# Attention and ternary feed-forward block on one core: x's first load in quarters, q rotated on VectorE alone, and the places of values steps, ring slots and inverse transfers

## What is computed

```python
q, k, v = n(x) @ Wq, n(x) @ Wk, n(x) @ Wv          # n: layer norm; 256, 64 and 64 columns
q = rope(q, ang); k = rope(k, ang[:, :8])          # q over its 256 columns, k within each head
p = softmax(einsum('bhqd,bhkd->bhqk', q, k) / 16)
x = x + n(einsum('bhqk,bhkd->bhqd', p, v) @ Wo)
w = where(W > d, 1, where(W < -d, -1, 0)) * alpha  # d = 0.7 * mean(abs(W))
x = x + n(n(x) @ w.T + bias)
```

## Time and profile before

| | |
|---|---|
| median of three runs | 1492.5 us (1488.67 to 1494.1) |
| profiled execution, its own time | 1492.92 us |
| its span, first to last instruction | 1491.1 us |
| TensorE matmul busy | 1431.0 us (96%) |
| VectorE busy | 1337.7 us (90%) |
| ScalarE busy | 1240.0 us (83%) |
| GpSimd busy | 754.6 us (51%) |
| first product of maxima begins | 49.28 us |

### The profile page before, as it was taken

The page is one execution under the profiler, slowest core; times in us unless marked ns, Lnnn a source line. Parts: engine busy times, 40 slices in busy tenths (PEclk is TensorE's granted clock), DMA queues, the critical chain, the costliest instruction groups (busy, mean ns, idle before and its releaser), DMA issues.

```text
span 1491.1 us, 32225 instructions
## 1 busy us (share of the span) xinstructions
PE 1431.0 (96%) x12350; PEld 460.7 (31%) x12350; DVE 1337.7 (90%) x1471; ACT 1240.0 (83%) x2483; POOL 754.6 (51%) x1205
## 2 busy tenths in 40 slices
PE   6699999999999999999999999999999999999996
PEld 5122322223232332323222233323322232222236
DVE  5798999999999999999999999999999989999814
ACT  2079889898988989898898989898898989899881
POOL 4322275645665466745656555745656455363340
PEclk9589999999999999999999999999999999999999
DMA  3311121311212130221313122221311112121001
GB/s 106 102 48 48 33 71 41 98 34 50 70 60 66 51 80 23 87 53 46 79 36 94 31 72 48 78 63 41 76 41 55 39 60 66 36 66 31 30 23 44
DMA packets 72921, 84.92 MB, mean 57 GB/s; under 512 B 17632, under 2 KB 58464, under 8 KB 71328
## 3 DMA queue, kind: packets, MB, share of 16 engines
q1 hardware_dynamic: 71952, 82.08, 19.7%
q10 hardware_dynamic: 816, 0.79, 0.2%
HBM read 46.66 MB, written 24.64 MB: 48 GB/s over the span
## 4 chain that ended last, share of the span: by engine, by line
PE 73%; ACT 12%; DVE 7%; issue 4%; POOL 2%; DMA 1%; SPq 0%; POOLq 0%; ACTq 0%; DVEq 0%
PE pv L1017 28%; PE smax L995 27%; ACT probs L887 10%; DVE row_max L1267 5%; PE ring L1130 5%; PE ring L1041 3%; PE ring L1104 3%; PE ring L1118 2%; PE ring L1138 2%; ACT heads L951 1%; PE ring L1124 1%; PE ring L1065 1%; PE ring L1088 1%; ACT act L940 1%; PE smax L961 0%
## 5 line engine op out<-in xcount | busy, mean ns | idle before, releaser
L1267 DVE TENSOR_REDUCE row_max<-smax 128x1 f32<-128x1024 f32 x1024 | 1202.0, 1216 | 82.6 <-PE smax L995 73.1
L887 ACT ACTIVATE probs<-ring 128x512 f32<-128x512 f32 x2048 | 1103.9, 598 | 114.2 <-PE ring L1041 91.7
L995 PE MATMUL smax<-k_rows,q_rows 48*128 48x512 f16 x2048 | 631.3, 389 | 14.4 <-DVE row_max L1267 5.9
L1041 PE MATMUL ring<-q_rows,k_rows 50*128 50x512 f16 x2048 | 637.6, 384 | 3.5 <-DMA q_rows<-max_rows 1.6
L1017 PE MATMUL pv<-probs,v_cols 128*32 128x256 f32 (+1 forms) x6520 | 610.8, 447 | 11.7 <-ACT heads L951 11.3
L995 PEld LDWEIGHTS smax<-k_rows,q_rows 48*128 48x128 f16 x2048 | 115.7, 94 | 493.4 <-issue 293.6
L1017 PEld LDWEIGHTS pv<-probs,v_cols 128*32 128x32 f32 x6520 | 128.7, 108 | 331.6 <-issue 180.9
L1041 PEld LDWEIGHTS ring<-q_rows,k_rows 50*128 50x128 f16 x2048 | 132.7, 93 | 54.8 <-ACT probs L887 46.3
L577 POOL TENSOR_TENSOR attnT<-pairs,inv_rows 128x512 f32<-128x512 f32 x31 | 39.5, 1273 | 178.6 <-DMA inv_rows<-inv_sums_dram 178.6
L556 POOL TENSOR_TENSOR act<-act,bias_sb 128x256 f32<-128x256 f32 x60 | 42.3, 728 | 115.4 <-ACT act L940 115.4
L1130 PE MATMUL ring<-wo_sb,attnT 128*128 128x256 f32 x256 | 72.2, 407 | 3.9 <-DVE attnT L577 1.7
(11 more groups left out here) (166 smaller groups left out, 1130.0 us busy)
## 6 DMA issues: line engine op xcount, KB each, us to landing
q_stage_dram<-q_parts SPq DMA_DIRECT2D x45, 256.0 KB, 2.5
q_rows<-q_stage_dram SPq DMA_DIRECT2D x30, 384.0 KB, 5.9
x_in<-in_L_attn_x SPq DMA_DIRECT2D x8, 1024.0 KB, 6.1
pairs<-heads SPq DMA_DIRECT2D x64, 128.0 KB
inv_rows<-inv_sums_dram SPq DMA_DIRECT2D x32, 256.0 KB
res<-in_L_attn_x SPq DMA_DIRECT2D x16, 512.0 KB, 4.2
out<-res SPq DMA_DIRECT2D x15, 512.0 KB, 3.2
k_rows<-k_stage_dram SPq DMA_DIRECT2D x64, 96.0 KB, 3.2
```

The lines of the kernel that those rows point to most:

```text
L887: eng.activation(probs[:, s % PSLOTS, j, :], ring[:, n % RING, :], ACT.Exp, scale=score_unit).then_inc(ring_read, 1)
L995: mm = eng.matmul(smax[:, side, c, :], q_rows[at:to, qc, kv * KVP + jp, qt * P:(qt + 1) * P], k_rows[at:to, kv, c * 512:(c + 1) * 512], st ...
L1041: eng.matmul(ring[:, n % RING, :], k_rows[at:to, g, kt * P:(kt + 1) * P], q_rows[at:to, h.qc, g * KVP + j // 2, :], start=True, stop=True)\
L1267: eng.tensor_reduce(row_max[:, g % 2, at:at + 1], smax[:, side, :, :].rearrange("p c n -> p (c n)"), AX.X, ALU.max).then_inc(max_read, 1)
```

## The change

Seven edits. x[0] is loaded in four transfers of two tiles, each with a semaphore, and VectorE's statistics wait tile by tile. TensorE starts on the first six constants, does 14 warming products, the weights' sums, then ten more, and only then waits for all constants. In the start VectorE rotates k and splits it, then does both halves of q's rotation; GpSimd waits until q is split and copies the values. The first q rows are loaded from ScalarE's queue, right behind q's staging; SP keeps the other q rows. SP's spreading of the inverses gets its own steps (5 and 23), behind the max-row transfers of step 5 and k's swaps of step 22. The ring's slots run on through all halves, and a slot is free when the read three before is done. In steps with transposes (XT, HT) the values go in halves after places 1 and 3, the job before them; steps 2, 10, 18 and 26 without a job get all values after place 2.

```diff
-INVERT, SCALED = {22: 0, 4: -1}, {27: 0, 7: -1}
+INVERT, SPREAD, SCALED = {22: 0, 4: -1}, {23: 0, 5: -1}, {27: 0, 7: -1}
+XT_TILES = 2
...
     def values_at(self, s):
-        return {3: ALL} if self.jobs_behind(s, 1) else {1: (0, 1), 3: (1, 2)}
+        kinds = [job[0] for job in self.jobs_behind(s, 1)]
+        if kinds and "XT" not in kinds and "HT" not in kinds:
+            return {3: ALL}
+        if not kinds and s % KT == LAG:
+            return {2: ALL}
+        return {1: (0, 1), 3: (1, 2)}
...
     def ring_free(self, n):
-        if n >= RING:
-            return self.base + n - RING + 1
-        return self.base - min(((count - n - 1) % RING for count in self.after), default=0)
+        return self.base + n - RING + 1
...
-            eng.dma_start(x_in[:, :, :], x[0, :, :].rearrange("(t p) d -> p t d", p=P)).then_inc(x_loaded, 16)
+            for n, done in enumerate(x_first):
+                at = n * XT_TILES
+                eng.dma_start(x_in[:, at:at + XT_TILES, :],
+                              x[0, at * P:(at + XT_TILES) * P, :].rearrange("(t p) d -> p t d", p=P)).then_inc(done, 16)
...
-            def spread_inverses(h, pair):
+            def store_inverses(h, pair):
                 eng.wait_ge(inverted, h.pair0 + pair + 1)
-                at_least(eng, divided, h.pair0 + pair)
                 eng.dma_start(inv_dram[pair % DT, :, :].rearrange("j (k n) -> (j k) n", n=FOLD),
                               inv_sums[:, pair % DT, :]).then_inc(inv_stored, 16)
+            def spread_inverses(h, pair):
+                at_least(eng, divided, h.pair0 + pair)
                 eng.wait_ge(inv_stored, (h.pair0 + pair + 1) * 16)
...
                     if s in INVERT and (h.scores if INVERT[s] >= 0 else h.flush):
-                        spread_inverses(h, INVERT[s])
+                        store_inverses(h, INVERT[s])
...
                                .then_inc(max_loaded, 16)
+                    if s in SPREAD and (h.scores if SPREAD[s] >= 0 else h.flush):
+                        spread_inverses(h, SPREAD[s])
...
                     take_k(0, 0)
-                    load_first_q()
+                    load_other_q()
...
                     if h.alone and h.pro is not None and s == Q_ROT_FIRST:
-                        rotate_first_q(eng, h, 1, ALU.add, rot_other)
                         eng.wait_ge(ring_read, h.done("V", 3))
+                        eng.wait_ge(parts_step, split_at(0, "Q0") + SPLIT_OPS[1])
...
+            def load_first_q():
+                eng.wait_ge(consts, CONSTS)
+                eng.wait_ge(q_staged[0], 16 * NBLK)
+                for side in range(2):
+                    eng.dma_start(q_rows[side * SIDE:side * SIDE + KROWS, 0, 0:KVP, :],
+                                  q_dram[0, :, :, side, 0:KVP, :].rearrange("m d h n -> (m d) h n"))\
+                       .then_inc(q_first, 16)
...
                         stage_first_q()
+                        load_first_q()
...
-                            eng.activation(probs[:, s % PSLOTS, j, :], ring[:, n % RING, :], ACT.Exp,
+                            eng.activation(probs[:, s % PSLOTS, j, :], ring[:, (h.base + n) % RING, :], ACT.Exp,
...
-            eng.wait_ge(consts, CONSTS)
+            eng.wait_ge(consts, CONSTS_FIRST)
...
             mm.then_inc(summed, 1)
+            warm(WARM_BEHIND)
+            eng.wait_ge(consts, CONSTS)
...
+                        if i == 1:
+                            n = projections(h, h.jobs_behind(s, i), n)
                         if i in parts:
                             values(h, s - LAG, *parts[i])
-                        n = projections(h, h.jobs_behind(s, i), n)
+                        if i != 1:
+                            n = projections(h, h.jobs_behind(s, i), n)
...
-                        if t == 0:
-                            eng.wait_ge(x_loaded, (h.mom + 1) * 16)
+                        if h.mom == 0:
+                            eng.wait_ge(x_first[t // XT_TILES], 16)
+                        elif t == 0:
+                            eng.wait_ge(x_loaded, h.mom * 16)
...
                         if s == Q_ROT_FIRST:
-                            rotate_first_q(eng, h, 0, ALU.subtract, rot_first)
                             rotate_first_k(eng, probs[:, 0, :, :], probs[:, 0, 2, :])
                             split_k(eng, 0, probs[:, 0, 2, :])
+                            rotate_first_q(eng, h, 0, ALU.subtract, rot_first)
+                            rotate_first_q(eng, h, 1, ALU.add, rot_other)
...
-WARM = 18
+WARM = 14
+WARM_BEHIND = 10
+CONSTS_FIRST = 6
```

More of the change, by code:

```diff
@@ L143, in __init__ @@
     def __init__(self, b, qc, scores=True, maxima=STEPS, turned=range(1, HKV + 1), pro=None, pro1=None,
-                 epi=None, late=None, rot=None, base=0, first=0, steps=STEPS, load_x=None, mom=None, flush=True,
-                 after=()):
+                 epi=None, late=None, rot=None, base=0, first=0, steps=STEPS, load_x=None, mom=None, flush=True):
         self.b, self.qc = b, qc
@@ L325, in sandwich_kernel @@
         x_loaded = sem("x_loaded")
+        x_first = [sem(f"x_first{n}") for n in range(KT // XT_TILES)]
         res_loaded = sem("res_loaded")
@@ L380, in schedule @@
             at += h.count
-            n0 = h.count
-            n1 = Half(0, 1, pro1=0, epi=(0, 0)).count
-            n2 = Half(0, 0, pro=0, epi=(0, 0)).count
             for b in range(B - 2):
[L385 to L392, removed]
+                h = Half(b, 1, pro1=b + 1, epi=(b, 0), late=(b - 1, 1) if b > 0 else None, rot=(b + 1, 0),
+                         base=at, mom=b + 2)
+                half(h)
+                at += h.count
+                h = Half(b + 1, 0, pro=b + 2, epi=(b, 1), late=(b, 0), rot=(b + 1, 1),
+                         base=at, load_x=b + 3 if b + 3 < B else None)
+                half(h)
+                at += h.count
+            h = Half(B - 2, 1, pro1=LAST, epi=(B - 2, 0), late=(B - 3, 1), rot=(LAST, 0), base=at)
             half(h)
             at += h.count
-            h = Half(LAST, 0, epi=(B - 2, 1), late=(B - 2, 0), rot=(LAST, 1), base=at, after=(h.count,))
+            h = Half(LAST, 0, epi=(B - 2, 1), late=(B - 2, 0), rot=(LAST, 1), base=at)
             half(h)
             at += h.count
-            h = Half(LAST, 1, epi=(LAST, 0), late=(B - 2, 1), maxima=STEPS - LEAD, turned=range(1, HKV), base=at,
-                     after=(h.count,))
+            h = Half(LAST, 1, epi=(LAST, 0), late=(B - 2, 1), maxima=STEPS - LEAD, turned=range(1, HKV), base=at)
             half(h)
             at += h.count
-            h = Half(B, 0, scores=False, maxima=0, turned=(), epi=(LAST, 1), late=(LAST, 0), base=at,
-                     after=(h.count,))
+            h = Half(B, 0, scores=False, maxima=0, turned=(), epi=(LAST, 1), late=(LAST, 0), base=at)
             half(h)
@@ L654, in stage_q, with load_other_q @@
                                   q_parts[:, part, :, qc, :]).then_inc(q_staged[qc], 16)
-            def load_first_q():
+            def load_other_q():
                 eng.wait_ge(q_staged[0], 16 * NBLK)
[L659 to L663, removed]
+                for side in range(2):
+                    eng.dma_start(q_rows[side * SIDE:side * SIDE + KROWS, 0, KVP:NPH, :],
+                                  q_dram[0, :, :, side, KVP:NPH, :].rearrange("m d h n -> (m d) h n"))\
+                       .then_inc(q_loaded[0], 16)
             def load_q(b, qc):
```

8 lines of the change are left out of this document (4 added, 4 removed).

## The result

| | before | after |
|---|---|---|
| median | 1491.12 us (4 runs) | 1508.79 us (3 runs) |
| profiled execution, its span | 1491.1 us | 1504.4 us |
| first reduction of maxima starts | 50.33 us | 44.42 us |
| last reduction of maxima starts, against before | | 13.6 us later |

The changed kernel is slower: ratio 1.0124 [1.0081, 1.0167], that is 18.5 us. Its profiled execution, 1506.25 us, is the shortest of its three runs, which go up to 1514.28. A fourth run, at 1705.3 us with a granted clock of 0.743 over its whole length, was disturbed and is left out everywhere.

A forecast was written before the change was run, and what follows sets the result against it. Nothing bulk runs before the first maxima; in the halves TensorE and VectorE are level, so either's wait counts. Terms -8.7 - 4.0 - 2.5 - 2.4 + 13.4 = -4.2 on 1492.9 gave 1488.7, so 1488 us; range 1477 to 1498.

The forecast's parts named there:

- the term of 13.4: Step 8: later spreading of the inverses makes WO wait for attnT, a loss of 13.4 us (0 to 16).
- my second rival: TensorE's clock falls in the new waits at step 8, some 1.7 us lost each; 1500 in all; chance 0.12.
- Values in the middle: 43 steps with whole values between VectorE's second unit's products; with other transposes, a gain of 2.5 us.
- VectorE is 0.31 behind at step 18: Walk through steps 17 to 28 of an even half: VectorE's delay at step 18, 0.31 us.
- the 0.17 ahead at step 28: End of the walk through an even half: VectorE 0.17 us ahead at step 28, counted 15 times.
- HT: Other transposes, 30 steps, before the feed-forward: 0.15 us gained each, 4.5 within the term of 2.5.
- my third rival: Values in the middle cost in full, VectorE bounding throughout: 11.3 us more than the term, 1499; chance 0.10.
- The start: Everything before the first maxima: they come at 40.5 us for 49.19, a gain of 8.7 us.
- q's rows take 3.2 to land: End of the start, after q's staging at 36.8: the rows land in 3.2 us, as in the kernel before.
- XT: Transposes of x, 24 steps in halves 2 to 12: 0.15 to 0.2 us a step, gain 4.0 (0 to 7).
- Ring: Start of a half: scores no longer wait for the previous half's last copy, gain 2.4 us (0 to 3.6).
- The rival that the four loads do not overlap: Start: x whole at about 14.8 us for 6.9, so the start gives 1 and the kernel 1496; chance 0.05.

The follow-up runs named there:

- e1: Changed kernel with the inverses spread at steps 4 and 22 again, right behind their store; ratio to before 0.9981, median 1487.7 us.
- e4: Kernel before with only the inverses' spreading moved to steps 5 and 23; ratio to before 1.0188.
- e13: e2 with SP loading the next batch's x at step 12 instead of 6; ratio to before 1.0044.
- e14: e4 with SP loading the next batch's x at step 12 instead of 6; ratio to before 1.0137.
- e7: e3 with SP's other q rows held back until the first q rows have landed; ratio to before 0.9871.
- e6: Changed kernel with only SP's other q rows held back until the first have landed; ratio to before 1.0126.
- e2: Changed kernel without whole values after place 2, those steps having halves after places 1 and 3; ratio to before 1.0093, median 1504.9 us.
- e3: Changed kernel with spreading back behind its store and no whole values after place 2; ratio to before 0.9885, median 1472.6 us.
- e9: e7 without the ten warming products behind the weights' sums; ratio to before 0.9874.

## Why the prediction was wrong

**The spreading: the term of 13.4, the step that failed most.** Place and mechanism were right: the spreading goes out behind the max rows, and `WO` waits for `attnT` in every half. The sum said 13.4, steps 8 and 9 measured 22.8. Two things were missing. The stall itself was nearly right in size: steps 8 without a fall take 5.25 to 5.48 in even halves with x's load, 2.0 to 2.5 more than before where I put 1.9; of that, some 1.6 is the new place (3.74 to 3.83 in e1), the rest that TensorE comes sooner. Odd halves lost 0.4 where I put 0.2; half 15, which I put at nothing, over 1 against e1. Without the falls it is about 15 in all. But the clock fell in three halves: 1.55 in half 2 (6.80 against 5.25) and, where it stayed down for 6.8 us, an estimated 2.7 each in halves 12 and 15 (7.60 against 4.93 in half 12 of e4, which waited as long and did not fall; 7.47 against 5.27 in half 15 of e13, less 0.5 for the longer wait there), 7 together. That was my second rival, with 0.12. Its price of 1.7 was right for a fall of 3.4 us and too low for the two of 6.8, and its chance was too low, although I had seen the same thing in half 15 of before; in the profiled executions of the versions with the later place it takes three to eight halves. And I counted what the new place is behind (max rows), not what comes right behind it on the queue: x's load, 2.12 away before and 0.69 after, which e13 and e14 price at 7.

**Values in the middle: wrong sign.** "VectorE is 0.31 behind at step 18" was 0.41, and the 0.17 ahead at step 28 never came. The steps where TensorE bounds give back only 0.1 to 0.2 each (steps 20, 27, 28), and steps 2 of odd halves, 10 of half 0 and all of half 15, which I had not followed, lose 0.4 to 0.8 with little given back. It cost 10.3, less the 1.1 of HT, where my third rival (0.10) had 8.8 for both. Two steps failed: the walk itself, which ends ahead where the steps show 0.1 lost in an even half, and carrying sixteen halves on a walk through twelve steps of one.

**The start: 5.9 for 8.7.** Right to 0.3 up to q's staging: split at 33.63 against 33.3, staged by 36.6 against 36.8. The failed term is "q's rows take 3.2 to land": the row of before was of a load that stood ahead of the other q rows and of six of the eight k loads on one queue. From ScalarE's queue it went out beside SP's 288 KB and 96 KB loads and took 5.3, for 2.3 in e7, which holds the q rows among them back. The Trainium skill ("DMA: Bandwidth & Descriptors", Issuing engines are not separate DMA queues) says that transfers of all issuing engines run on the same 16 engines and interleave, and that another issuing engine saves only issue time; I used the second half of that and called the move worth nothing. The landings of 5.3 and 2.3 agree with the first half. Not holding SP's loads back cost 2.9 (e6); what the move itself cost against the load kept on SP was not run. And of the 5.9 about 2 are the luck of the two profiles, as the starts above show. The floor that I named, the last product of q ending at 40.4, became real in e7 (40.53).

**Right.** XT: 4.7 for 4.0. Ring: 3 to 4 for 2.4. f32 products of 0.69 and the upper clock level for k and for q up to its last products, which run from 38.04 at the lower one. The rival that the four loads do not overlap is refuted: their last landing is at 6.87, for 6.89 in one transfer, so that staying under the 1 MiB a transfer that the Trainium skill ("DMA: Bandwidth & Descriptors", Rules for kernel authors) gives for full bandwidth cost nothing here. HT: right sign, 1.1 for 4.5.

So the two rivals on the slower side, 0.22 together, both happened at once, and I had treated them as exclusive: 9.4 more for the spreading, 8.3 for the middle, 3.4 for HT and 2.8 for the start, less 2.3 in ring and XT and 3.8 in the rest, are the 17.8 between -4.2 and 13.6. That the runs are 18.5 slower and the profiled execution 13.6 is the spread of the changed kernel's runs, of which that one had few falls.

## What to carry to other kernels

A transfer moved back in an engine's list must be read with its new neighbours on both sides, the large load right behind it above all; and an urgent transfer on a second queue can land late beside what the first queue sends (5.3 for 2.3 us here), so let the others wait for it. In a kernel where TensorE and VectorE are level, a new wait of TensorE (1.6 us and more here) can cost its length and a stretch at the lower clock besides; make a forecast with and without it, and let rivals add up. Where falls of the clock come and go, read how often from the granted clock of every run, not from one profile. Check a reordering inside a step on every kind of half, since what a later step gives back depends on which engine bounds it.

## What the runs showed of the hardware that I had not expected

- Waits of the same length do and do not bring the clock down: `WO` in the changed kernel waited 2.13 in half 2 (lower level from 266.2 on) and 2.15 in half 4 (clock stays at 1.00); 1.84 in half 12 was followed by 6.8 us at the lower level. The changed kernel passed waits up to 2.38 unhurt, and e1 fell in half 14 after 0.99 and 0.90. The number of halves hit was 3, 7, 8, 6, 6 and 5 in the profiled executions of the changed kernel, e6, e2, e4, e13 and e14, and the changed kernel's times spread over 8 us where e3's, with none, spread over 0.8.
- The 256 KB of inverses took 3.50 to 3.78 us from issue to use in e13's even halves 2 to 10, with no load beside them, 3.98 to 4.31 in e2's with 1 MiB issued 0.7 behind. Ahead of `WO` in the other halves of the same executions, which have no such load in either, it was 3.56 to 4.01. Three times they took much longer: 6.42 in half 4 and 4.68 in half 10 of e4 with the load, and 4.68 in half 4 of e14 without it, which no run explains.
- A start made late by the lower clock is not made up: in its profiled execution e9 begins 3.3 later than e7, with 10.2 us at the lower level from 9.8 on, and its last reduction starts 3.1 later. The medians are 1.7 apart.
